# First feed-forward of a two-layer fp4/ternary network on one core: the scales of coming inputs and the side work stand behind the residual, and the first tile of a pass has no statistics or norms of later chunks

## The reference

```python
x = x + 0.5 * _L0_ffn_ref(_layernorm(x), w_gate, w_up, w_down)
x = x + _L0_attn_ref(_layernorm(x), ...)          # gated linear attention
x = x + 0.5 * _L0_ffn_ref(_layernorm(x), w_gate, w_up, w_down)
x = x + 0.5 * _L1_ffn_ref(_layernorm(x), ...)     # ternary weights
x = x + _L1_attn_ref(_layernorm(x), ...)
x = x + 0.5 * _L1_ffn_ref(_layernorm(x), ...)
```

```python
def fp4_linear(x, w):                 # both quantised and scaled back
    return einsum('bsk,nk->bsn', fp4_quant_dequant(x), fp4_quant_dequant(w))
gate = fp4_linear(x, w_gate)          # 256 -> 704
y = fp4_linear(x, w_up)               # 256 -> 704
h = silu(gate) * y
return fp4_linear(h, w_down)          # 704 -> 256
```

## Time and profile before

| what | value |
|---|---|
| time, median of 3 runs | 2712.8 us (2710.54 to 2718.06) |
| the profiled execution's own time | 2717.34 us |
| its span | 2715.3 us |
| PE busy | 2511.8 us, 93% |
| DVE busy | 1867.3 us, 69% |
| ACT busy | 1408.5 us, 52% |
| POOL busy | 1273.5 us, 47% |

### The profile page before, as it was taken

How to read it: one execution, slowest core, us unless ns; L and a number is a source line. 1 busy time by engine, 2 the same in 40 slices (tenths; PEclk the granted TensorE clock), 3 DMA queues, 4 the chain that set the end, 5 groups by cost and what they waited for, 6 DMA issues and landing times.

```text
span 2715.3 us, 78014 instructions
## 1 busy us (share of the span) xinstructions
PE 2511.8 (93%) x32232; PEld 2169.1 (80%) x32232; DVE 1867.3 (69%) x4324; ACT 1408.5 (52%) x2345; POOL 1273.5 (47%) x1382
## 2 busy tenths in 40 slices
PE   4999999999999989988999899989999999979999
PEld 3878888778888868777888788878888888858888
DVE  8888888657777788888887466645556565645664
ACT  3545555434333335544554688864444544418886
POOL 5877787611111147767877333311444434462221
PEclk8999999989999999999999899999999999989999
DMA  5000000001001010000000000000000000000001
GB/s 177 2 7 1 1 1 1 1 16 24 23 23 23 23 45 1 1 1 1 1 1 1 17 1 1 1 9 19 17 17 19 17 16 17 17 6 24 32 32 40
DMA packets 67566, 45.97 MB, mean 17 GB/s; under 512 B 13184, under 2 KB 66192, under 8 KB 67216
## 3 DMA queue, kind: packets, MB, share of 16 engines
q1 hardware_dynamic: 67216, 41.00, 5.4%
HBM read 15.78 MB, written 8.40 MB: 9 GB/s over the span
## 4 chain that ended last, share of the span: by engine, by line
PE 63%; issue 16%; POOL 11%; DVE 4%; ACT 4%; DMA 0%; SPq 0%; POOLq 0%; DVEq 0%; ACTq 0%
PE ps L46 12%; PE ps L47 10%; PE ps L48 10%; PE ps L1458 4%; PE ps L1459 4%; PE ps L1475 3%; PE ps L1473 3%; PE ps L608 3%; PE ps L1007 2%; PE ps L264 2%; PE ps L1095 2%; DVE XTL L274 2%; POOL a1pry L2027 2%; POOL a1pry L2029 2%; POOL a1l L2015 2%
## 5 line engine op out<-in xcount | busy, mean ns | idle before, releaser
L1525 DVE TENSOR_TENSOR gHl<-gHf,gHh 128x512 fp32r<-128x512 f32 x256 | 190.9, 746 | 210.2 <-ACT gHh L1502 209.8
L46 PE MATMUL ps<-WGH,XTH 128*128 128x512 f32 (+1 forms) x768 | 314.8, 410 | 14.9 <-ACT fSG L660 13.4
L231 POOL TENSOR_SCALAR ve<-mv 128x4 f32<-128x4 f32 x96 | 23.5, 245 | 635.7 <-DVE mv L221 631.8
L48 PE MATMUL ps<-WGL,XTH 128*128 128x512 f32 (+1 forms) x768 | 291.7, 380 | 0.0
L47 PE MATMUL ps<-WGH,XTL 128*128 128x512 f32 (+1 forms) x768 | 291.3, 379 | 0.0
L660 ACT ACTIVATE fSG<-ps 128x704 f32<-128x704 f32 x128 | 97.0, 758 | 368.2 <-PE ps L48 368.1
L779 POOL TENSOR_TENSOR fHTL<-fHTF,fHTH 128x768 fp32r<-128x768 f32 x128 | 235.7, 1841 | 107.3 <-ACT fHTF L669 107.0
L1473 PE MATMUL ps<-W2T,gHh 128*128 128x256 f32 x1024 | 256.2, 283 | 0.0
L1475 PE MATMUL ps<-W2T,gHl 128*128 128x256 f32 x1024 | 253.7, 282 | 0.0
L46 PE MATMUL ps<-WDH,fHTH 128*128 128x256 f32 (+1 forms) x768 | 241.2, 314 | 12.3 <-issue 11.1
L1458 PE MATMUL ps<-XTH,W1T 128*128 128x512 f32 x512 | 206.4, 403 | 21.4 <-DVE XTL L274 18.8
(11 more groups left out here) (237 smaller groups left out, 7104.4 us busy)
## 6 DMA issues: line engine op xcount, KB each, us to landing
X<-in_x SPq DMA_DIRECT2D x16, 512.0 KB, 8.8
a0vp<-a0vt SPq DMA_DIRECT2D x256, 32.0 KB, 2.3
a1vp<-a1vk SPq DMA_DIRECT2D x256, 32.0 KB, 2.3
out<-X SPq DMA_DIRECT2D x16, 512.0 KB, 2.9
tws<-in_w SPq DMA_DIRECT2D x2, 1024.0 KB, 7.7
WN<-in_wgu SPq DMA_DIRECT2D x3, 384.0 KB, 5.7
a0km<-in_wqkv SPq DMA_DIRECT2D x2, 384.0 KB, 3.4
a1pry<-in_aw SPq DMA_DIRECT2D x1, 768.0 KB, 4.5
```

The source lines that it names most:

```text
L46: e.matmul(o, hh, mh, start=first, stop=False)
L48: return e.matmul(o, hh, ml, start=False, stop=last)
L1525: dve.tensor_tensor(Hl[m % 8][:, :], Hf[m % 4][:, :], Hh[m % 8][:, :].bitcast(F32), ALU.subtract).then_inc(s_hl, 1)
```

## The change

On DVE `x_scale` of chunk i+2 moves from behind `hidden(n)` to behind the residual, and so do the set steps (all but the step of iteration 21, which the code keeps ahead of the residual because PE waits for it). The maxima `xam` move from bank 2 to bank 5 of PSUM. The wait of PE for `s_qxsn` goes; instead ACT waits for it ahead of the magnitudes in iterations with j = 2. The statistics of chunk 2 are made before the pass, with its `spread`; those of chunk 3 are made in iterations 1 and 2, and its `spread` in iteration 2 of POOL, behind `x_value`. ACT makes the norm of chunk 2 in iteration 1, behind the magnitudes of tile 0. POOL's memsets for the attention block wait for that earlier `spread`. No instruction is added or removed.

```diff
-        xam = lambda S, i: QT[0][:, 0, 0:64] if S and i == 0 else PS[3][:, 0:64] if i < 2 else PS[2][:, 428:492]
+        xam = lambda S, i: QT[0][:, 0, 0:64] if S and i == 0 else PS[3][:, 0:64] if i < 2 else PS[5][:, 256:320]
...
         def before_dve(dve):
             dve.memset(PSA[64:128, 3712:3840], 0.0).then_inc(s_hz, 1)
             x_scale(dve, 2, 1)
+            for k in range(8):
+                stats(dve, 2, 2, k)
 
         def before_pool(pool):
             x_value(pool, 2, 1)
+            spread(pool, 2, 2)
...
             x_scale(dve, 0, 1)
+            for k in range(8):
+                stats(dve, 0, 2, k)
...
             x_value(pool, 0, 1)
+            spread(pool, 0, 2)
...
                 if n and c == 2:
                     pe.wait_ge(s_hsn, t)
-                    if n % 4 == 2 and n // 4 + 2 < NS:
-                        pe.wait_ge(s_qxsn, 8 * S + n // 4 + 3)
...
+                    if j == 2 and i + 2 < NS:
+                        act.wait_ge(s_qxsn, 8 * S + i + 3)
                     act.activation(mag.bitcast(R32), V[(n - 1) % 2][:, :], ACT.Abs, scale=MAGIC).then_inc(s_ha, 1)
...
-                    if n == 0:
-                        norm(act, S, 2, (0, 1))
-                    if j == 0 and i + 2 <= NS:
+                    if n == 1:
+                        norm(act, S, 2)
+                    if j == 0 and n and i + 2 <= NS:
                         norm(act, *chunk(16 * S + i + 2), (2, 3))
...
-                if n == 0:
-                    for k in range(8):
-                        stats(dve, S, 2, k)
-                    for k in range(4):
-                        stats(dve, S, 3, k)
-                if j == 0 and i + 3 <= NS + 1:
+                if j == 0 and n and i + 3 <= NS + 1:
...
-                if n % 4 == 1 and n // 4 + 2 < NS:
-                    x_scale(dve, S, n // 4 + 2)
...
-                if n in when0 and S == 0:
-                    attn0_set_dve(dve, when0.index(n))
-                if n in when1 and S == 2:
-                    ffn1_set_dve(dve, when1.index(n))
+                if n == when1[9] and S == 2:
+                    ffn1_set_dve(dve, 9)
                 if n >= 4:
                     dve.wait_ge(s_dn, t - 3)
                     dve.scalar_tensor_tensor(out=X[:, n - 4, :], in0=down, scalar=0.5,
                                              in1=X[:, n - 4, :], op0=ALU.mult, op1=ALU.add).then_inc(s_xd, 1)
+                if n % 4 == 1 and n // 4 + 2 < NS:
+                    x_scale(dve, S, n // 4 + 2)
+                if n in (1, 2):
+                    for k in range(4 * n - 4, 4 * n):
+                        stats(dve, S, 3, k)
+                if n in when0 and S == 0:
+                    attn0_set_dve(dve, when0.index(n))
+                if n in when1 and n != when1[9] and S == 2:
+                    ffn1_set_dve(dve, when1.index(n))
...
-                if n == 0:
-                    spread(pool, S, 2)
...
-                if n < NT and j == 1 and i + 3 <= NS + 1:
+                if n < NT and j == 1 and n > 1 and i + 3 <= NS + 1:
                     spread(pool, *chunk(16 * S + i + 3))
...
+                if n == 2:
+                    spread(pool, S, 3)
...
-            pool.wait_ge(s_qxv, 2)
+            pool.wait_ge(s_nb, 6)
```

## The result

The changed kernel takes 2679.28 us (median of 4 runs, 2675.49 to 2685.58) against 2711.89 for the kernel before (4 runs). The ratio is 0.9878, with a 95% interval of 0.9853 to 0.9902: 32.6 us faster, clearly outside the 0.3%. Forecast were 2661 us and the range 2651 to 2676. The sign was right; the forecast gain of 51.5 us was too large, and the time lies 3 us above the range.

A forecast was written before the change was run, and what follows sets the result against it. PE was taken as the bound (busy 93%), its idle time as what can be won. 10.8 + 10.6 + 9.3 + 4.8 + 2.3 + 8.4 + 2.5 + 2.8 = 51.5 us gave 2661 us, range 2651 to 2676.

The forecast's parts named there:

- The clean gaps: PE's waits ahead of the hidden's turn in undisturbed iterations go: 10.8 us in the first pass, 10.6 in the second.
- The rival by which DVE becomes the bound in each group: In groups of four tiles DVE's thin slack runs out, 15 us of gain are lost: 2676 us, chance 12%.
- The new wait: ACT's wait for `s_qxsn` ahead of the magnitudes in j = 2 costs nothing, with 1.4 us to spare.
- The starts: At each pass start the silu no longer waits behind the norm: 2.5 us gained in the first pass, 2.8 in the second.
- the start pays nothing: Rival: at pass starts, statistics delay the first product or DVE's chain eats the gain: 2666 to 2671 us, chance 15%.
- The set steps: Iterations 9 to 19 of the first pass gain 9.3 us; 8 to 15, 21 and 24 to 31 of the second 4.8, 2.3, 8.4.
- With DVE never waiting they take 2 x 34.7 = 69.4 us: Iterations 24 to 31, second pass: DVE becomes the bound, two groups fall from 77.8 to 69.4 us, gaining 8.4 us.
- Each has a step of 2.19 us: Iterations 24 to 31, second pass: each set step keeps DVE busy 2.19 us, as read in the profile before.
- 2.3 us: Iteration 21, second pass: PE's 5.1 us wait for DVE's step shrinks without 2.07 us of `x_scale` ahead; gain 2.3 us.
- no more can be had, as the order alone changes: Iterations 24 to 31, second pass: the gain cannot exceed 8.4 us, the stage not fall below 69.4 us.

The follow-up runs named there:

- the repeat: The changed kernel measured once more, unchanged, against the kernel before: 2674.06 us, ratio 0.9866.
- the doubled comparison: Changed kernel with the comparison done twice in each set step of iterations 24 to 31 of the second pass: 2688.95 us, ratio 0.9899 to the kernel before.
- the spread-out steps: Changed kernel with set steps in odd iterations where POOL is idle: 2654.84 us (0.9789); with iteration 21's down product also ahead of PE's wait, 2655.39 us (0.9781).

## Why the prediction had the sign right and the gain 14 to 19 us too large

**The clean gaps (10.8 and 10.6 us): right.** The passes save 19.2 and 20.2 us; less what the starts save by tile 5 (2.1 and 3.2) and the set groups (6.2, and 3.9 + 0.4 + 2.1), 10.9 and 10.6 us are left. In iteration 41 of the changed kernel, on DVE:

```profile
351.95 0.41 DVE L764 SCALAR_TENSOR_TENSOR X<-ps,X 128x256 f32<-128x256 f32 x1
352.28 1.22 DVE L325 TENSOR_REDUCE ps<-XN 128x64 f32<-128x1024 f32 x1
...
355.20 0.89 DVE L729 TENSOR_TENSOR fH<-ps,fSG 128x704 f32<-128x704 f32 x1 [0.18 <-issue]
```

The residual ends at 352.36 and PE's turn starts at 353.23, so it has 0.9 us to spare, and DVE is ready for the next gated product 0.18 us early; forecast were 0.9 and 0.2. The rival by which DVE becomes the bound in each group is refuted: tiles follow at 7.0, 7.5, 7.5, 7.0 us. Its time, 2676 us, lies nearest to the measured one of all rivals, but by chance: none of the clean gaps came back.

**The new wait: right but for a trifle.** ACT waits for it once in each pass, in iteration 2, where the start of the pass still holds DVE: 1.5 us in the first and 0.9 in the second. In the first pass:

```profile
ACT ps L680 <- DVE fxsc L328: 1.5, 1, 1.5
```

**The starts (2.5 and 2.8 us): right.** In the second pass, on ACT:

```profile
974.10 0.74 ACT L664 ACTIVATE fSG<-ps 128x704 f32<-128x704 f32 x1
974.73 0.75 ACT L680 ACTIVATE ps<-fV 128x704 fp32r<-128x704 f32 x1
975.41 2.06 ACT L251 ACTIVATE XN<-X,nb,rs 128x256 f32<-128x256 f32 x4
```

The silu comes ahead of the norm, and PE's first gap is 1.51 us (forecast near 1.5) instead of 6.66. From the gated product of tile 0 to that of tile 3 it takes 990.07 - 969.57 = 20.5 us instead of 23.8, 3.3 us less; in the first pass it is 2.1 us less, and 3.2 in the repeat. The kernel with this part alone saves 3.2 us by tile 5 in each pass, so "the start pays nothing" falls. One reading is to be set right: before, the granted clock fell not behind PE's gap of 6.66 us but 2.0 us into it (at 995.44), and stayed at 1.2 GHz until 1005.68. With the gap of 1.51 us it did not fall at the start of the second pass, which the prediction had called possible and had not counted.

**The set steps: wrong, and the only step that failed.** Forecast were 9.3 + 4.8 + 2.3 + 8.4 = 24.8 us, measured in two profiles 6.2 + 3.9 + 0.4 (or -0.8) + 2.1 = 11.4 to 12.6 us. Half of the miss is one sentence, the first of these three.

- "With DVE never waiting they take 2 x 34.7 = 69.4 us". DVE's own work came out as forecast, 68.5 us. (The 26.0 us of other work in a group stand in no row, give 25.4; the eight steps took 18.7 us and not 17.5. The two errors partly cancel.) But DVE waited 7.2 us of the 75.7. The steps now stood ahead of the next inputs, and PE waited 4.1 us for POOL's L361 and 4.1 us for DVE's L274; the down product and the residual came late, and the granted clock was at its lower level for 13.7 us. I had looked at what stands behind the residual, not at who waits for the `inputs` behind the moved steps. Behind the inputs, the wait for L361 shrinks to 1.6 us, 5.9 us come back, and the stage takes 69.7 us.
- "Each has a step of 2.19 us". A duration that holds only in one phase against POOL was used in another. The steps took between 1.14 and 3.82 us each. In the sum that is small (18.7 against 17.9 us before), but the two steps of 3.8 us are what L274, and PE behind it, waited for in iterations 26 and 30. In the first pass another one grew likewise: L904 of 0.95 us, twice, is L910 now and takes 2.03 each time. Iterations 10 and 11, where it stands, take 8.4 and 8.1 us, 7.6 each before, and in iterations 13 and 17 PE waits 1.4 us for L361. Most of the 3.1 us by which that group missed lies in these four iterations; no run parts the longer operation from its place ahead of the inputs. That it is POOL's work beside a step that stretches it is shown by the doubled comparison and, from the other side, by the steps in POOL's idle time at 1.14 to 1.2 us.
- "2.3 us" for iteration 21. The wait shrank as computed, but the stretch at the lower clock behind its end grew from 3.1 us to 6.8, and to 9.4 in the repeat, and took 1.9 to 3.1 us back. The prediction counted nothing for it. Why the clock falls in some kernels and not in others stays open.

I had also called 69.4 us a floor ("no more can be had, as the order alone changes"). With the spread-out steps the same iterations take 58.5 us. That is a different plan, with half the steps inside them, but iterations 32 to 39, which take the rest, need 51.1 us against 50.8: the steps cost nothing there.

Of the difference of 18.9 us between the forecast gain and the first measurement, the set steps explain 12 to 13. The remaining 6 are in no stage of the passes; the medians, unlike the two profiled executions, simply lie no further apart than 32.6 us. Against the second measurement (37.3 us) the forecast is 14 us too large.

## What to carry to other kernels

A duration read in a trace belongs to its place: before an operation of VectorE with SBUF inputs is moved, look at what GpSimd runs at the new place, and put it where GpSimd is idle, or ahead of its start. When a step is moved on an in-order engine, follow both neighbours: who waits for the work that it no longer delays, and who waits for the work that it now delays. Side work of equal pieces is best spread one piece to each slack of its size (here every second iteration), which took iterations 24 to 31 from 15 us of idle PE in the kernel before to none; a single long wait can be filled by putting ready work of the same engine ahead of it (3.07 us became 0.63).

## What the runs showed of the hardware that I had not expected

- One VectorE comparison of 128x512 fp32 takes 0.39 us with GpSimd idle, and 1.50 or 2.04 us when it starts within an operation of GpSimd of 1.39 or 2.12 us. The other way round GpSimd's L791 of 1.39 us took 1.56 in the kernel before, when the comparison had started 0.16 us ahead of it.
- With the same wait of PE of 3.07 or 3.08 us, the granted clock did not fall in one kernel, fell 1.1 or 1.4 us behind its end in two, and during it in four. The stage takes 10.9 us with the wait and without the fall, and 12.3 to 15.1 with both: the fall costs 1.4 to 4.2 us, up to more than the 2.6 us of the wait. Without either it takes 8.3.
- A wait as short as 1.93 us was followed by the lower clock: in iteration 25 of the changed kernel it ended at 1158.76, and from 1160.16 on PE ran at 1.2 GHz for 6.8 us.
